# Layer 1's weights loaded straight from DRAM in small transfers, and another order at the start

## The reference, cut to what matters

```python
inputs = emb[feature_ids] * feature_vals[:, :, None]          # 1024 x 39 fields x 16
input_biases = bias_emb[feature_ids][..., 0] * feature_vals
h = inputs
for i in range(3):                                            # CIN layers of 200 outputs
    x = einsum('bhd,bmd->bhmd', h, inputs).reshape(B, -1, 16)  # all pairs (h, field)
    x = relu(einsum('bcd,oc->bod', x, W[i]) + b[i][None, :, None])
    h, direct = (x[:, :100], x[:, 100:]) if i != 2 else (h, x)
    finals.append(direct)
cin_result = sum(concatenate(finals, axis=1), axis=-1)
d = relu(relu(inputs.reshape(B, -1) @ W0.T + b0) @ W1.T + b1)  # 624 -> 400 -> 400
out = (concatenate((cin_result, d), axis=1) @ fc_W.T + fc_b)[:, 0] + sum(input_biases, axis=1)
```

## Time and profile before

| | us |
|---|---|
| median of 3 runs | 2761.99 (2759.05 to 2763.11) |
| the profiled execution, whole | 2760.82 |
| its span, from the first to the last instruction | 2759.0 |
| PE busy | 2648.8 |
| PE's first matmul with weights starts at | 83.57 |
| layer 1's weights landed, ACT goes on at | 65.10 |
| layer 2's weights landed, ACT goes on at | 122.37 |

### The profile page before, as it was taken

How to read it: one execution, slowest core, us unless ns; L and a number is a source line. 1 busy time by engine, 2 the same in 40 slices (tenths; PEclk the granted TensorE clock), 3 DMA queues, 4 the chain that set the end, 5 groups by cost and what they waited for, 6 DMA issues and landing times.

```text
span 2759.0 us, 66659 instructions
## 1 busy us (share of the span) xinstructions
PE 2648.8 (96%) x17928; PEld 2639.4 (96%) x17928; DVE 2277.2 (83%) x4580; ACT 1834.7 (66%) x4774; POOL 2248.6 (82%) x1912
## 2 busy tenths in 40 slices
PE   0599999999999999999999999999999999999999
PEld 0599999999999999999999999999999999999998
DVE  1688888888888888888888888888888888888884
ACT  0467666766767667677666777677666776776663
POOL 5788888888888888888888888888888888876763
PEclk9899999999999999999999999999999999999999
DMA  8744454545545454454544445444454445544441
GB/s 157 175 131 119 125 142 115 138 114 132 136 118 132 117 142 126 118 137 111 147 121 125 132 124 138 117 130 126 129 137 113 136 119 136 131 116 131 115 114 52
DMA packets 199913, 349.82 MB, mean 127 GB/s; under 512 B 66631, under 2 KB 118696, under 8 KB 199614
## 3 DMA queue, kind: packets, MB, share of 16 engines
q1 hardware_dynamic: 181758, 339.69, 44.6%
q0 software_dynamic: 10496, 2.88, 3.0%
q10 hardware_dynamic: 7488, 5.80, 0.7%
HBM read 344.29 MB, written 14.17 MB: 130 GB/s over the span
## 4 chain that ended last, share of the span: by engine, by line
PE 94%; SPq 3%; issue 1%; DVE 1%; DMA 1%; POOL 0%; ACT 0%; POOLq 0%; ACTq 0%; DVEq 0%
PE acc L626 61%; PE acc L627 28%; PE acc L653 2%; PE hrep L664 1%; SPq L320 1%; SPq L310 1%; DMA odd<-lin 0%; DVE W L1026 0%; PE acc L719 0%; PE acc L718 0%; PE acc L720 0%; SPq L322 0%; SPq L325 0%; PE hrep L740 0%; PE hrep L742 0%
## 5 line engine op out<-in xcount | busy, mean ns | idle before, releaser
L626 PE MATMUL acc<-W,xhi_d 128*128 128x400 f32 x5632 | 1731.9, 367 | 11.0 <-DVE xlo_d L1052 9.6
L627 PE MATMUL acc<-W,xlo_d 128*128 128x200 f32 x5632 | 1435.0, 255 | 0.0
L1052 DVE TENSOR_TENSOR xlo_d<-prod_d,xhi_d 128x512 fp32r<-128x512 f32 (+1 forms) x1536 | 982.2, 640 | 210.0 <-ACT xhi_d L795 144.4
L1044 DVE TENSOR_TENSOR prod_d<-hrep,xrep 128x512 f32<-128x512 f32 (+1 forms) x1536 | 1038.7, 677 | 108.9 <-ACT hrep L837 33.8
L548 POOL TENSOR_TENSOR xlo_p<-prod_p,xhi_p 128x512 fp32r<-128x512 f32 (+1 forms) x768 | 954.1, 1242 | 171.8 <-ACT xhi_p L789 119.6
L627 PEld LDWEIGHTS acc<-W,xlo_d 128*128 128x128 f32 x5632 | 1078.4, 191 | 0.0
L626 PEld LDWEIGHTS acc<-W,xhi_d 128*128 128x128 f32 x5632 | 1059.6, 188 | 13.4 <-DVE xlo_d L1052 11.5
L795 ACT ACTIVATE xhi_d<-prod_d 128x512 fp32r<-128x512 f32 (+1 forms) x1536 | 885.0, 577 | 217.9 <-PE acc L627 199.5
L626 PE MATMUL acc<-W,xhi_p 128*128 128x400 f32 x2944 | 916.6, 363 | 12.0 <-POOL xlo_p L548 12.0
L542 POOL TENSOR_TENSOR prod_p<-hrep_s,xrep 128x512 f32<-128x512 f32 x512 | 666.9, 1303 | 167.2 <-ACT hrep_s L832 121.5
L627 PE MATMUL acc<-W,xlo_p 128*128 128x200 f32 x2944 | 751.1, 255 | 0.0
(11 more groups left out here) (92 smaller groups left out, 918.9 us busy)
## 6 DMA issues: line engine op xcount, KB each, us to landing
xrep<-xs SPq DMA_DIRECT2D x384, 384.0 KB
l0x<-xs SPq DMA_DIRECT2D x378, 136.5 KB
xrep<-xs SPq DMA_DIRECT2D x384, 128.0 KB
xrep<-xs SPq DMA_DIRECT2D x128, 336.0 KB
xrep<-xs SPq DMA_DIRECT2D x128, 64.0 KB
l0x<-xs SPq DMA_DIRECT2D x378, 19.5 KB
raw<-table,idx POOLq DMA_INDIRECT x328
W<-lin SPq DMA_DIRECT2D x2, 2100.0 KB
```

Of the source, the lines that this page charges most:

```text
L626: pe.matmul(bank[:, 0:2 * OUTS], hi, w, start=first, stop=last, skip_group_check=True)
L627: return pe.matmul(bank[:, 0:OUTS], lo, w[:, 0:OUTS], start=False, stop=last, skip_group_check=True)
L1044: nc.vector.tensor_tensor(to, h, xrep[:, (par + layer - 1) % 2, a:a + count, :], ALU.mult).then_inc(s_prod_d, 1)
L1052: op = nc.vector.tensor_tensor(xlo_d[:, slot, 0:split], bank[:, 0:split], xhi_d[:, slot, 0:split].bitcast(F32), ALU.subtract)
```

## The change

Layer 1's weights are loaded by SP straight into a raw buffer in `xrep`, by 110 transfers: 84 runs of `count` tiles in four partitions (one of each quarter), and 26 for the rest. To make four partitions one transfer, the h's of layer 0's result are put in another order when ACT takes them: partition 32e + 8q + g holds h 25q + 8e + g. Layer 2's copy into `lin2` goes from ACT to SP, behind the first blocks. Layers 1 and 2 are split in five pieces; POOL makes the low half of one of layer 1's. The rows of tile 0 are scaled ahead of the split of layer 1's weights, four embedding columns first. The raw layer 0 weights and the second chunk's pairs move to `prod_p`; since raw weights now lie in `xrep`, its rows of ones are set after the split, and the loads of blocks wait for them (`s_ones`). Step 1's pieces of layer 2 are split after D4 to D8 instead of D3 to D6. Step 0 is written out.

```diff
+            for m in range(FIELDS):
+                if m < M_MAIN - 1:
+                    at[m] = (QUARTER * e + g, m)
+                elif m >= M_MAIN:
+                    at[m] = (H_MAIN + g, BLOCK_M * e + m - M_MAIN)
...
-        PIECES = [[(0, KT[0])]] + 2 * [[(8, 16), (0, 8), (16, ODD), (ODD, KT[1])]]
-        W_DONE = [1, 5, 9]
+        PIECES = [[(0, KT[0])]] + 2 * [[(8, 16), (0, 8), (16, 24), (24, ODD), (ODD, KT[1])]]
+        W_DONE = [1, 6, 11]
...
-        W2_AT = {3: 0, 4: 1, 5: 2, 6: 3}
-        W2_NEEDED = {("D", 6): 6, ("P", 4): 7, ("D", 8): 8, ("D", 11): 9}
+        W2_AT = {4: 0, 5: 1, 6: 2, 7: 3, 8: 4}
...
+            for first, count, part, tile in W1_RUNS:
+                to = raw1[part:part // QUARTER * QUARTER + QUARTER:8, tile:tile + count, :]
+                load(to.rearrange("p k o -> p (k o)"), rows_at(first, [[step, 4], [row, count]]))
+            last = 24 * FIELDS
+            for t in range(4):
+                for j, count in ((0, 6), (6, 2)):
+                    load(raw1[H_MAIN + 4 * j:H_MAIN + 4 * (j + count), SPARE + t, :],
+                         rows_at(last + 4 * j + t, [[4 * row, count], [step, 4]]))
+            engine.wait_ge(s_pad, 1)
...
+                    load(raw1[part:part // QUARTER * QUARTER + QUARTER:8, LAST_T, :],
+                         rows_at((8 * e + g) * FIELDS + M_MAIN - 1, [[step, 4]]))
...
-            rows_of_weights(sp, 1, w1)
+            load_weights1(sp)
             sp.dma_start(fcw[:], fc_w.partition_broadcast(P)).then_inc(s_fc, 16)
             sp.dma_start(fcb[:], fc_b.partition_broadcast(P)).then_inc(s_fc, 16)
-            sp.wait_ge(s_pad, 1)
-            load_weights(sp, 1, w1)
...
             sp.wait_ge(s_x0, 128)
-            sp.wait_ge(s_wlo, W_DONE[0])
+            sp.wait_ge(s_ones, 1)
             for e in (1, 2, 0, 3):
                 load_block(0, 0, e)
-            sp.wait_ge(s_pt, 4)
+            rows_of_weights(sp, 2, w2)
             sp.wait_ge(s_prod_p, p_num(0, 1) + 1)
             load_layer0(2)
+            sp.wait_ge(s_ones, 2)
...
+            a, b = PIECES[1][1]
+            pool.wait_ge(s_whi, 3)
+            nc.gpsimd.tensor_tensor(weights(1)[:, a:b, 1, :], raw_weights(1, a, b),
+                                    weights(1)[:, a:b, 0, :].bitcast(F32), ALU.subtract).then_inc(s_wlo1, 1)
...
+                if l == 0:
+                    by_q = h.rearrange("p (q k) -> p q k", q=4)
+                    nc.scalar.activation(hbuf[l][:, 0:H_MAIN].rearrange("p (e q g) -> p e q g", e=3, q=4),
+                                         by_q[:, :, 0:24].rearrange("p q (e g) -> p e q g", e=3), ACT.Relu)
...
-            rows_of_weights(act, 2, w2)
...
+            def set_ones(buf):
+                dve.wait_ge(s_wlo, 3 + 2 * buf)
+                for t in (SPARE + 4, LAST_T):
+                    op = nc.vector.memset(xrep[H_MAIN:P, buf, t, :], 1.0)
+                op.then_inc(s_ones, 1)
```

More of the change, by code:

```diff
@@ L82, in step_order @@
 def step_order(i):
[L84 to L87, removed]
+    return [g for g in ORDER if layer_of(*g) in present(i)]
 def p_num(i, k):
@@ L112, in d_bank, with w1_runs @@
     return d_num(i, d) % BANKS if isinstance(i, int) else d % BANKS
+def w1_runs():
+    runs = []
+    for k in range(24):
+        e, g = k // 8, k % 8
+        at = {}
+        for m in range(FIELDS):
[3 more added lines that the diff above has]
+                at[m] = (H_MAIN + g, BLOCK_M * e + m - M_MAIN)
+            else:
+                at[m] = (QUARTER * e + g, LAST_T) if e < 2 else (H_MAIN + g, LAST_T - 1)
+        for m in range(FIELDS):
+            r = k * FIELDS + m
+            if runs and r % QUARTER and runs[-1][4] == k and at[m] == (runs[-1][2], runs[-1][3] + runs[-1][1]):
+                runs[-1][1] += 1
+            else:
+                runs.append([r, 1, *at[m], k])
+    return [tuple(r[0:4]) for r in runs]
+W1_RUNS = w1_runs()
 def some(n):
@@ L274, in raw_weights @@
                 return raw0[0][:, a:b, :]
+            if layer == 1:
+                return raw1[:, a:b, :]
             if a >= ODD:
@@ L585, in _ @@
             copy_idx(1, 1)
-            pool.wait_ge(s_xin, 3)
[L587 to L591, removed]
+            product(-1, 1, 0)
+            pool.wait_ge(s_pt, 4)
+            product(-1, 1, 1)
+            low(-1, 0)
+            low(-1, 1)
+            product(0, 0, 0)
+            product(0, 0, 1)
+            low(0, 0)
+            low(0, 1)
+            pool.wait_ge(s_xin, 3)
+            for m in range(4):
+                gather(m)
+            product(0, 0, 2)
+            product(0, 0, 3)
+            low(0, 2)
+            for m in range(4, 7):
+                gather(m)
+            product(1, 1, 0)
+            low(0, 3)
+            for m in range(7, 9):
+                gather(m)
+            step(1, 1, 0, range(9, BEFORE))
             with pool.Fori(0, TILES - 1) as k:
@@ L643, in multiply @@
                     pe.wait_ge((s_hbuf[0], s_hbuf[1], s_dot[2])[layer], c)
[L644 to L647, removed]
+                if isinstance(i, int) and c == 0 and (kind, g) in W_NEEDED[layer]:
+                    pe.wait_ge(*W_NEEDED[layer][(kind, g)])
                 for n, t in enumerate(tiles):
@@ L698, in _ @@
             first_inputs(1, (prod_d[2], acc[2]))
-            step(-1)
-            step(0)
+            multiply(-1, "P", 0)
+            multiply(-1, "P", 1)
+            turn(0, 0, -1)
+            multiply(0, "P", 0)
+            multiply(0, "P", 1)
+            multiply(0, "D", 0)
+            multiply(0, "D", 1)
+            multiply(0, "P", 2)
+            multiply(0, "D", 2)
+            multiply(0, "D", 3)
+            turn(0, 1, 0)
+            multiply(0, "D", 4)
+            multiply(0, "D", 5)
+            multiply(0, "P", 3)
             step(1)
@@ L844, in step @@
                 layers = present(i)
-                inner = not (isinstance(i, int) and i < 1)
                 p_groups = p_groups_of(i)
@@ L863, in step @@
                         low_copy(0, i + 1, i)
-                    if (kind, g) == ("P", 3) and layers == (0, 1):
-                        take(0, i + 1)
-                        spread(0, i + 1, i)
                     if (kind, g) == ("D", 6) and 0 in layers:
@@ L910, in _ @@
                 split_weights(1, n)
-            rows_of_weights(act, 2, w2)
             high(-1, "P", 0)
-            step(-1)
-            step(0)
+            high(-1, "P", 1)
+            high(0, "P", 0)
+            low_copy(0, 0, -1)
+            take(0, 0)
+            spread(0, 0, -1)
+            high(0, "P", 1)
+            high(0, "D", 0)
+            high(0, "D", 1)
+            high(0, "P", 2)
+            low_copy(0, 1, 0)
+            high(0, "D", 2)
+            high(0, "D", 3)
+            take(0, 1)
+            high(0, "P", 3)
+            high(0, "D", 4)
+            high(0, "D", 5)
+            spread(0, 1, 0)
+            high(1, "P", 0)
             step(1)
@@ L1088, in step @@
                         evacuate(0, i + 1)
+                    if d == 0 and isinstance(i, int) and i == 1:
+                        evacuate(1, 0)
                     if d == 9 and 1 in layers and 0 in layers:
@@ L1113, in _ @@
             product(0, 0, 1)
-            step(0, 0, [])
+            product(0, 0, 2)
+            low(0, 0)
+            split_weights(1, [3])
+            product(0, 0, 3)
+            low(0, 1)
+            split_weights(1, [4])
+            set_ones(1)
+            product(0, 0, 4)
+            low(0, 2)
+            evacuate(0, 1)
+            product(0, 0, 5)
+            low(0, 3)
+            low(0, 4)
+            low(0, 5)
             product(1, 1, 0)
```

117 lines of the change are left out of this document (70 added, 47 removed).

## The result

| | before | after |
|---|---|---|
| median, us | 2763.11 (5 runs) | 2799.63 (5 runs, 2792.96 to 2801.68) |
| profiled execution | 2760.82 | 2801.68 |
| its span | 2759.0 | 2799.6 |

The changed kernel is slower: ratio 1.0132, 95% interval 1.012 to 1.0143. The direction was right. The size was not, 36.5 us instead of 15, outside the range.

What follows compares the result with a forecast made beforehand. PE bounds the kernel at 96% busy, so only its entry into the steady stretch moves, set by W1's and W2's landings. 2760.8 + 17.7 (W2 later) - 1.5 = 2777.0, then 1.2 to the median: 2778 us, range 2757 to 2793.

Steps and rivals of the forecast that it cites:

- Where the time is decided.: Start of the kernel: landings of W1 (65.1 before) and W2 (122.3 before) set when PE enters its unchanged steady stretch.
- 1.5 us expected behind W2: Step 1 after W2 lands: splits start one group later, so PE waits less; gain of 1.5 us, 0 to 3.
- Four engines, always the same.: W1's direct load: outermost count 4 puts all transfers on the same four DMA engines, 989 rows each at 40 ns.
- SP's 26 last issues of about 0.42 us: End of W1's load: the last 26 transfers cost SP 10.9 us, some 4 hidden, so W1 lands at 84 or 85.
- rival 1: W1's load: the four engines change between transfers, W1 lands at about 56, time 2754 us (2750 to 2758); chance 0.13.
- L: Time at which W1 lands: 65.1 us before the change, forecast 84, 19 us later.
- The gathers hold the engines at 51.9%.: W1's load, 10 to 60 us: gathers take 51.9% of all DMA engines, leaving 24 us an engine for rows.
- bounds of 60 to 95: W1's landing: about 60 to 65 if gathers take no engine time, 95 if they take 60% and rows more time.
- L to the first blocks, 7.3.: W1's landing to first block load: waits for split pieces and ones, 7.3 us; 9.6 us gained against L.
- The blocks to W2.: First blocks to W2's landing: W2's rows on SP add 9 us; W2 lands at L+56 against L+57.2 before.
- h in its new order, 0.: ACT's take of h from PSUM, strided, 250 ns before: no time cost expected, a loss possible.
- Rival 2: W1's load: four engines not held by gathers, W1 lands at 62 to 72, end 2757 to 2767; chance 0.10.

Runs made afterwards that it cites:

- e6: Changed kernel with 44 of W1's 110 transfers on ACT's queue and the first gathers started only once W1 has landed; 2805.2 us, one execution.
- e4: Changed kernel with POOL waiting for layer 1's weights before its 39 gathers; 2830.5 us, one execution, only W1's landing to be read.
- e17: Changed kernel with a small POOL write and a wait for it behind each of the first 39 gathers; 2777.2 us, one execution.
- e18: Changed kernel with 44 W1 transfers and W2's rows on ACT's queue, second ones early, a small POOL write behind each gather; 2757.61 us, ratio 0.9987.
- e19: Changed kernel with 44 W1 transfers and W2's rows on ACT's queue, second ones early, a small write behind every second gather; 2753.13 us, ratio 0.9966.

## Why the prediction was wrong, step by step

- *Where the time is decided.* Right: two landings, and the steady part untouched. From W2's split to the end it was 2636.6 us before and 2637.2 after. Of the 1.5 us expected behind W2 nothing is seen, though the runs scatter around 2636 by more than that.
- *Four engines, always the same.* It fits (e6), and had little weight: from 33.9 on, and in all of e4 behind layer 0's weights, they weren't the bound.
- ***SP's 26 last issues of about 0.42 us, and no word of the other 84.* This is the step that failed.** The forecast charges SP only for these 26, and rival 1, the one place that counts all 110, takes 0.42 us for each too (48 us). 0.42 us is what the transfers over 128 partitions took; one with a count of 4 holds the queue for 0.63, and the next comes 0.67 after it. The kernel before had shown it: in the earlier trace rows itself L333, with its count of 2, takes 0.60. And so do rows of SP's timeline and of the chain that I didn't read for this:

```profile
54.04 3.87 SPq L325 DMA_DIRECT2D W<-lin  x4
57.95 0.81 SPq L327 DMA_DIRECT2D odd<-lin  x1
58.80 0.41 SPq L330 DMA_DIRECT2D odd<-w  x1
57.27 0.64 SPq L325
```

  Four of count 8 in 3.87 us, the shortest of them in 0.64, one of count 7 in 0.81, and a single row in 0.41. Even by the 0.64, with 0.04 between two, 110 issues take 75 us, and with 1.7 ahead W1 cannot land before 77; the sum would have been made from SP, not from the engines. It measured 79.2 with the gathers away (e4) and 80.0 beside spaced ones (e17). With this step alone put right L would have come out near 77, below the 84 of the forecast; what puts the time outside the range is the next one.
- ***The gathers hold the engines at 51.9%.* This step failed too, and it puts the time outside the range.** Up to 33.9 something of the kind is there: the engines stand at 0.88, SP is held, and the changed kernel has 35 issues out where e4 has 46 and e17 44. That is some 7 us. After that it is wrong in kind: rows wait for SP and not SP for rows, the share is 0.30 and less, and the gathers still cost 17 us, by slowing SP's issues from one in 0.67 to one in 1.68 us. In e17 all the gathers run beside W1 and cost 0.8 us in all. Nothing in the trace of before shows the slowing, for there SP had few issues in that time and waited for landings. So L = 84 stood near e17's 80.0 by two errors that pulled against each other (engines too slow, issues too cheap), which is luck, and the bounds of 60 to 95 held no case for 103. Spelt out, with e4 and e17 of one execution each: 65.1 + 14.1 (issues) + 0.8 (spaced gathers beside them) + 23.0 (gathers without a pause: 6 before 33.9, 17 behind it) = 103.0.
- *L to the first blocks, 7.3.* It measured 9.1 (103.0 to 112.1). ACT's part held; DVE's second piece took 4.09 us beside POOL's of 3.79, where 1.8 was taken. Its first piece, of the same size and alone, took 1.83. The scaling was done long before L, as said (first at 56.2, since the gathers were in 4 us before the 60.4 taken), and POOL's first lower half came at L + 11. DVE's two pieces, POOL's, and what POOL did next:

```profile
104.59 1.83 DVE L1138 TENSOR_TENSOR W<-xrep,W 128x1600 fp32r<-128x1600 f32 x1 [43.66 <-ACT W L874]
107.44 4.09 DVE L1138 TENSOR_TENSOR W<-xrep,W 128x1600 fp32r<-128x1600 f32 x1 [1.03 <-ACT W L874]
106.07 3.79 POOL L651 TENSOR_TENSOR W<-xrep,W 128x1600 fp32r<-128x1600 f32 x1 [51.98 <-ACT W L874]
109.78 1.83 POOL L559 COPY idx<-idi 128x39 int32<-128x39 int32 x1
```

- *The blocks to W2.* From the first block to `load_weights` 24.2 us (112.09 to 136.33), as summed, and W2's rows took 9.7 where I took 9. W2's split came at L + 59.4 instead of 56: 1.8 from the step before, and the rest in the issue and landing of W2 itself, 26.0 instead of 24.5.
- *h in its new order, 0.* Right. The take stayed at 251 ns, as in the earlier trace rows:

```profile
L911 ACT ACTIVATE hbuf<-acc x128: 251/252/253, 121.1 to 2702.4; 128x96 f32<-128x96 f32 x128
```

- *Rival 1* (W1 at 56) didn't come, and e6 speaks against its reason; e18 splits W1 at 55.8, but with two queues, which is another kernel. *Rival 2* (L at 62 to 72) said that gathers don't hold the engines, which is so only behind 33.9, and the bound of the issues (79.2) stood behind it.

The sum, corrected: 2760.8 + 37.9 (L) + 2.1 (59.4 instead of 57.3 from L to W2's split) = 2800.8, against 2801.7.

## What to carry to other kernels

Count the issues before the bytes: so many transfers times the queue's time for one of that shape, taken from a row of a transfer of the same outermost count, is a bound of its own. When a transfer is cut up, spread the pieces over two queues from the start, and look whether indirect transfers run beside them back to back. Before a gain is claimed for such a kernel, load it more than once, and on more than one chip.

## What the runs showed of the hardware that I had not expected

- A transfer with an outermost count of 4 costs its queue 0.63 us, 0.67 with the gap, whether it moves 4 rows or 124 (the last sixteen, with one row for each partition, 0.58); with 24 or 28 rows over as many partitions 0.74 to 0.79; a single row 0.42, like a wide transfer. The Trainium skill ("DMA: Bandwidth & Descriptors", section "Why a DMA increments its semaphore by 16 and not by 1") says that the issuing sequencer writes the part of the 16 increments that the engines don't. One could expect from it that narrow ones are dearer, which fits 0.63 against 0.42. The 0.42 of the single row speaks against this as the whole reason; no run here settles it.
- Gathers issued by POOL at one in 1.25 us slowed SP's and ACT's queues to about 1.7 us a turn after 20 to 30 of them, and until 11 to 19 us after the last; at 1.44 us (e17, e18) and at 1.35 on the mean (e19), with a wait on POOL between them, they didn't. Two loads of the same code, on two chips, differed by 19 us in this.
- POOL's and DVE's subtractions of the same size took 3.79 and 4.09 us side by side; DVE's alone took 1.83. POOL's was not longer than the 3.9 that the forecast took for it, and DVE's was done 1.7 us behind it, at 111.53. The small copy that POOL did meanwhile took 1.83 us, where the earlier trace rows has 0.21, and was done at 111.61. So it looks as if each held the other up in turn, and not as if both ran slower; no run takes POOL's piece away to test it.
